# A two-layer decoder on one core: the opening's loads, one store, four transposes and the logarithm parts are moved

## The reference

```python
# layer 0, state space:   u = (x W_in2' + b) * sigmoid(x W_gate' + b_gate);  h_t = h_{t-1} A' + u_t B';  y = h C';  out = y W_out' + b_out
# layer 0, cross attention over 64 context tokens, 16 heads, with a mask
# layer 0, linear:        tanh(x W A1 A2 + bias)
# layer 1, local attention: scores from the cosine of g = x Wg' + bg, window of 128 tokens,
#     weighted with 1 / (mean + 0.5), softmax, times v = x Wv' + bv, then Wo
# layer 1, strided cross attention (4 keys a head)
# layer 1, feed forward: silu(q(x) q(Wg)') * (q(x) q(Wu)'), times q(Wd)', with q = rounding to 4-bit floats in blocks of 16
```

## Time and profile before

| | |
|---|---|
| median of 3 runs | 2803.29 us (2802.55 to 2804.59) |
| profiled execution | 2801.17 us |
| its span | 2799.6 us |
| PE busy | 2630.1 us (94%) |
| DVE, ACT, POOL busy | 1907.7, 808.7, 865.4 us |
| mean granted clock of PE | 0.978 |
| first stage | about 2 to 408 us |
| second stage | about 409 to 927 us |
| local attention | about 928 to 1600 us |

### The profile page before, as it was taken

One profiled execution on the slowest core, in us unless ns is written; L12 is line 12 of the kernel. 1 busy time (PEld: TensorE's weight loads), 2 busy tenths in 40 slices (PEclk: granted clock), 3 DMA queues, 4 the chain that ended last, 5 costly groups with the idle time before them and its releaser, 6 DMA issues. The chain is left out here.

```text
span 2799.6 us, 36866 instructions
## 1 busy us (share of the span) xinstructions
PE 2630.1 (94%) x13006; PEld 1586.6 (57%) x13006; DVE 1907.7 (68%) x3304; ACT 808.7 (29%) x1193; POOL 865.4 (31%) x902
## 2 busy tenths in 40 slices
PE   7999988999998889999998679999999999999996
PEld 3444534555555444444444346777777777777774
DVE  3688403666667336666678658888888888888884
ACT  1111312333332246666668511111111111111110
POOL 1232103554554346666667501111111111111000
PEclk9999989999999999999999989999999999999998
DMA  5344130000000133333335501111111111111111
GB/s 161 118 164 173 49 112 14 1 1 1 1 1 1 54 104 93 87 95 92 99 101 147 159 27 41 43 44 43 43 43 43 43 44 43 43 44 44 40 38 34
DMA packets 219395, 176.91 MB, mean 63 GB/s; under 512 B 38319, under 2 KB 184111, under 8 KB 218190
## 3 DMA queue, kind: packets, MB, share of 16 engines
q1 hardware_dynamic: 182230, 147.85, 17.6%
q10 hardware_dynamic: 36984, 26.71, 3.5%
HBM read 90.51 MB, written 52.43 MB: 51 GB/s over the span
## 5 line engine op out<-in xcount | busy, mean ns | idle before, releaser
L2016 PE MATMUL bank<-tiles,tl_XQT 128*128 128x512 f32 (+1 forms) x768 | 331.8, 575 | 7.6 <-DMA tl_XQT<-tl_QB 4.9
L2031 PE MATMUL bank<-tiles,tl_HT 128*128 128x512 f32 x704 | 316.3, 605 | 19.7 <-DMA tl_HT<-tl_tmp 19.7
L2021 PE MATMUL bank<-tiles,tl_XQT 128*128 128x512 f32 (+1 forms) x768 | 318.0, 557 | 0.0
L2031 PEld LDWEIGHTS bank<-tiles,tl_HT 128*128 128x128 f32 x704 | 225.2, 324 | 95.3 <-issue 28.0
L2016 PEld LDWEIGHTS bank<-tiles,tl_XQT 128*128 128x128 f32 x768 | 232.5, 310 | 74.0 <-issue 16.4
L2021 PEld LDWEIGHTS bank<-tiles,tl_XQT 128*128 128x128 f32 x768 | 236.7, 308 | 65.6 <-issue 0.2
L1376 POOL TENSOR_SCALAR_AFFINE_SELECT tiles<-tiles 128x512 f32<-128x512 f32 x256 | 179.5, 704 | 202.6 <-ACT tiles L1595 187.2
L1969 POOL TENSOR_TENSOR tl_rs<-tl_ve,mhalf 128x1 f32<-128x1 f32 x32 | 17.6, 549 | 593.0 <-DVE tl_ve L2124 593.0
L2065 ACT ACTIVATE tl_HQ<-bank 128x512 f32<-128x512 f32 (+1 forms) x96 | 53.9, 562 | 427.7 <-PE bank L2016 406.3
L1702 DVE SCALAR_TENSOR_TENSOR tiles<-tiles,bank 128x1024 f32<-128x1024 f32 (+1 forms) x128 | 141.7, 1148 | 25.2 <-PE bank L1475 25.2
L1381 POOL TENSOR_SCALAR_AFFINE_SELECT tiles<-tiles 128x512 f32<-128x512 f32 x224 | 152.6, 681 | 0.0
(11 more groups left out here) (279 smaller groups left out, 4961.1 us busy)
## 6 DMA issues: line engine op xcount, KB each, us to landing
tl_HT<-tl_tmp SPq DMA_DIRECT2D x256, 44.0 KB, 1.9
tl_HT<-tl_tmp ACTq DMA_DIRECT2D x256, 44.0 KB, 2.0
fp_weights<-space_quant ACTq DMA_DIRECT2D x33, 256.0 KB, 2.2
X<-in_x SPq DMA_DIRECT2D x8, 1024.0 KB, 12.0
v<-tiles SPq DMA_DIRECT2D x32, 256.0 KB, 2.4
unit_g<-tiles SPq DMA_DIRECT2D x32, 256.0 KB, 2.4
unit_gT<-tiles SPq DMA_DIRECT2D x32, 256.0 KB, 2.8
la_GN<-unit_g SPq DMA_DIRECT2D x128, 64.0 KB, 2.0
```

The source lines that it names most:

```text
L2016: mm = e.matmul(bank[(2 * q) % 3][:, 0:w], chunk(XQT[n % 2], c), WgT[q][:, :, c, :], start=(c == 0), stop=(c == C - 1))
L2021: mm = e.matmul(bank[(2 * q + 1) % 3][:, 0:w], chunk(XQT[n % 2], c), WuT[q][:, :, c, :], start=(c == 0), stop=(c == C - 1))
L2031: mm = e.matmul(bank[DOWN][:, :], chunk(HT, q), WdT[:, q, :], start=(q == 0), stop=(q == IC - 1))
```

## The change

It has five parts. In the first stage, the small loads, the output weights and the five bias columns move from ACT's queue to SP's: Bm and the small loads before the first FP4 unit, the others behind it, before x. The gate weights and the input weights are loaded in halves of 256 columns with a semaphore each, the gate weights' second half behind the two biases. The second folded store signals a kept semaphore, and SP waits for it in the second stage, just before it loads the local attention's weights. The transposes of the first four tiles of x go to banks 0 to 3, and only those from the sixth tile on wait for a copy. In the local attention `y_parts` goes from part 0 of its round to part 1 of the next, behind `norms`.

```diff
             def _(e):                                   # first stage, SP
                 e.dma_start(xT[0][:, :, :].rearrange("p c t -> p (c t)"), a["x_T"][0]).then_inc(s_xt[0].sem, 16)
-                e.dma_start(WiT[:, :, :], chunked(a["L0_attn_W_in_T"])[:, :, D:2 * D]).then_inc(s_wi.sem, 16)
+                for h in range(2):
+                    e.dma_start(WiT[:, :, h * D // 2:(h + 1) * D // 2],
+                                chunked(a["L0_attn_W_in_T"])[:, :, D + h * D // 2:D + (h + 1) * D // 2]).then_inc(s_wi[h].sem, 16)
                 e.dma_start(xT[1][:, :, :].rearrange("p c t -> p (c t)"), a["x_T"][1]).then_inc(s_xt[1].sem, 16)
...
+                e.wait_ge(s_zero.sem, s_zero.at(4))
+                e.dma_start(BmP[:, :, 0:ST], chunked(a["L0_attn_Bm_T"])).then_inc(s_bm.sem, 16)
+                for b in range(B):
+                    q = slice(QB * b, QB * b + ST)
+                    e.dma_start(Pw[0][q, q], a["L0_attn_A"]).then_inc(s_small.sem, 16)
+                    e.dma_start(PwT[0][q, q], a["L0_attn_A_T"]).then_inc(s_small.sem, 16)
+                    e.dma_start(CmP[:, :, q], chunked(a["L0_attn_Cm"])).then_inc(s_small.sem, 16)
                 load_weights(0)
+                e.dma_start(WoT[:, :, :], chunked(a["L0_attn_W_out_T"])).then_inc(s_wo.sem, 16)
+                for t, n in ((bk, "L0_xattn_bk"), (bq5, "L1_xattn_bq"), (bk5, "L1_xattn_bk"), (bv5, "L1_xattn_bv"), (lbv, "L1_attn_bv")):
+                    e.dma_start(t[:, :], columns_of(a[n]), allow_slow_non_contiguous=True).then_inc(s_cols.sem, 16)
                 for g in GROUPS:
...
-                e.dma_start(k.SW[:, VO_AT:FOLDED], w.VB).then_inc(s_out.sem, 16)
-                e.wait_ge(s_out.sem, s_out.at(32))
+                e.dma_start(k.SW[:, VO_AT:FOLDED], w.VB).then_inc(k.d_folded, 16)
+                e.wait_ge(s_out.sem, s_out.at(16))
...
-                    if g == 0 and m == 0:               # gate; inputs() likewise
-                        e.wait_ge(s_wg.sem, s_wg.at(16))
+                    if g == 0 and m % 2 == 0:
+                        e.wait_ge(s_wg[m // 2].sem, s_wg[m // 2].at(16))
...
             def _(e):                                   # first stage, ACT
-                e.dma_start(WgT[:, :, :], chunked(a["L0_attn_W_gate_T"])).then_inc(s_wg.sem, 16)
+                def gate_weights(h):
+                    x = slice(h * D // 2, (h + 1) * D // 2)
+                    e.dma_start(WgT[:, :, x], chunked(a["L0_attn_W_gate_T"])[:, :, x]).then_inc(s_wg[h].sem, 16)
+
+                gate_weights(0)
                 e.dma_start(bg[:, :], ...)              # and bi, as before
+                gate_weights(1)
                 e.wait_ge(s_bias.sem, s_bias.at(16 * 2))
...
+        x_bank = lambda n: n if n < B else XTB           # second stage
...
+                e.wait_ge(k.d_folded, 16)
                 e.dma_start(WgT[:, :, :], chunked(a["L1_attn_Wg_T"])).then_inc(s_next.sem, 16)
...
                 def transpose_x(n):
                     e.wait_ge(s_xe.sem, s_xe.at(n - 11))
-                    e.wait_ge(s_tc.sem, s_tc.at(n))
-                    transposed(x_tile(n), s_t)
+                    if n > B:
+                        e.wait_ge(s_tc.sem, s_tc.at(n))
+                    transposed(x_bank(n), x_tile(n), s_t)
...
+                    if part == 1 and batch_of(m) is not None:   # local attention, DVE, behind norms(m)
+                        y_parts(batch_of(m))
...
                     if part == 0:
                         if tile(m - 1):
                             unit(m - 1)
-                        b = batch_of(m)
-                        if b is not None:
-                            y_parts(b)
                         if tile(m):
                             biased(m)
```

More of the change, by code:

```diff
@@ L74, in __init__ @@
         self.done = []
+        self.d_folded = self.kept("folded_stored")
         self.d_w, self.d_wd = [self.kept(f"ffn_w{q}") for q in range(len(PIECES))], self.kept("ffn_w_down")
@@ L249, in ssm_and_weight_products @@
         bk, bq5, bk5, bv5, lbv = (sb(n, [P, C]) for n in ("bk", "bq5", "bk5", "bv5", "lbv"))
-        s_zero, s_const, s_small, s_wg, s_wi, s_bm, s_wo = (sem(n) for n in (
-            "zero", "one_row_made", "small", "w_gate", "w_in", "w_Bm", "w_out"))
+        s_zero, s_const, s_small, s_bm, s_wo = (sem(n) for n in ("zero", "one_row_made", "small", "w_Bm", "w_out"))
+        s_wg, s_wi = ([sem(f"w_{n}{h}") for h in range(2)] for n in ("gate", "in"))
         s_xt, s_x = [sem(f"xT_load{p}") for p in range(2)], [sem(f"x_load{g}") for g in GROUPS]
@@ L411, in inputs @@
                     e.wait_ge(s_u.sem, s_u.at(C * g + m - 1))
-                    if g == 0 and m == 0:
-                        e.wait_ge(s_wi.sem, s_wi.at(16))
+                    if g == 0 and m % 2 == 0:
+                        e.wait_ge(s_wi[m // 2].sem, s_wi[m // 2].at(16))
                     for c in range(C):
@@ L935, in _, with transposed @@
             def _(e):
-                def transposed(src, done):
+                def transposed(to, src, done):
                     for c in range(C):
-                        mm = e.transpose(bank[XTB][:, c * P:(c + 1) * P], src[:, c * P:(c + 1) * P], k.ident[:, :])
+                        mm = e.transpose(bank[to][:, c * P:(c + 1) * P], src[:, c * P:(c + 1) * P], k.ident[:, :])
                     mm.then_inc(done.sem, 1)
@@ L949, in transpose_x2 @@
                     e.wait_ge(s_xe.sem, s_xe.at(n))
-                    transposed(x_tile(n), s_xl)
+                    transposed(XTB, x_tile(n), s_xl)
                 def query(i):
@@ L1034, in _ @@
                         e.wait_ge(s_q.sem, s_q.at(C * (n // B - 1)))
-                        e.activation(XT[(n // B) % 2][:, :, (n % B) * P:(n % B + 1) * P], four(bank[XTB][:, :]), ACT.Copy).then_inc(s_tc.sem, 1)
+                        e.activation(XT[(n // B) % 2][:, :, (n % B) * P:(n % B + 1) * P], four(bank[x_bank(n)][:, :]), ACT.Copy).then_inc(s_tc.sem, 1)
                     if there(s - 2):
```

10 lines of the change are left out of this document (removed).

## The result

| | before | after |
|---|---|---|
| median of 4 runs each | 2802.92 us (2802.51 to 2804.59) | 2767.53 us (2766.48 to 2768.41) |
| profiled execution | 2801.17 us | 2768.34 us |
| its span | 2799.6 us | 2766.4 us |
| mean granted clock | 0.978 | 0.983 |

The ratio is 0.9872, with a 95% interval of 0.9855 to 0.989. The change is 35.4 us faster by the medians, where 28 was forecast. The direction was right and the size too small.

What follows compares the result with a forecast made beforehand. PE, nearly always busy, was taken to bound the kernel, other engines counting only where it waits. Gains 10.5 + 3.1 + 3.7 + 1.0 + 9.7 = 28.0 us led to 2775 us (own range 2770 to 2781; 8 in 10: 2769 to 2783).

Steps and rivals of the forecast that it cites:

- Opening: Start of the first stage: ACT's shorter queue and halved weights bring the third gate group earlier; gain 10.5 us (7 to 12).
- Store: First stage boundary: the end of the stage no longer waits for the last folded store; gain 3.1 us (2.7 to 3.4).
- Banks: Start of the second stage: transposes 1 to 4 need no copy before them; gain 3.7 us (3.2 to 4.2).
- Clock term: First query group of the second stage: the clock may rise near its start; gain 1.0 us (−0.3 to 2.1).
- Batches 1 and 2: Local attention: dots start 4.1 us earlier and 1.1 to 1.2 more is saved behind them; gain 5.3 us per batch.
- Batch 0: Local attention: PE's transposing would wait for the logarithm steps, ready only behind the norms; −0.9 us (−2 to 0).
- Batch 3: Local attention: steps and DVE's inverse only change order, PE waits as now for the scaled tile; 0 us (−1 to 1).
- The logarithm parts as a whole: Local attention, all four batches: moving the steps a round later gains 9.7 us (6 to 12).
- A: Opening: SP's queue becomes the limit as ACT's was, the opening gains 4 us, time 2782; chance 0.13.
- B: Local attention: the logarithm parts give nothing, this part gains 1 us, time 2784; chance 0.08.
- C: Whole kernel: steadier PE load lowers the granted clock; no gain from 1.1% less, 2814 at 1.5%; chance 0.03.
- D: Opening: bytes decide it, so it isn't earlier and gains 0, time 2786; chance 0.04.

Runs made afterwards that it cites:

- filled_transposes: Changed kernel with the first five tiles transposed through one bank again, plus four unread transposes behind each of these tiles; 2772.31 us.
- old_opening: Changed kernel with only the opening put back as before (small loads on ACT's queue, whole gate and input weights); 2779.76 us.
- fp4_first: Changed kernel with the first unit of the FP4 weights issued ahead of Bm and the small loads; 2768.38 us.
- filled_dots: Changed kernel with the logarithm steps early again, PE doing four overwritten 128x512 products where it would stand in batches 1 and 2; 2778.71 us.
- late_12: Changed kernel with the logarithm steps late in batches 1 and 2 only, in the old place in batches 0 and 3; 2771.47 us.
- y_early: Changed kernel with DVE's seven logarithm steps back in their old place in front of the bias addition; 2780.26 us.
- quarters_fp4: Changed kernel with gate and input weights in quarters instead of halves and the first FP4 unit ahead of the small loads; 2766.21 us.

## Why the prediction was right and where it was wrong

- **Opening, right.** Forecast: first gate group at 10.8, third at 28.3; measured 10.66 and 28.56, 11.0 gained (forecast 10.5). The first gate group took 6.32 where 5.4 was counted. SP's queue was quicker than counted (last small load at 16.00, forecast 18.9; FP4 weights at 21.6, forecast 23 to 24), so most of the 0.8 taken off for a late u or a late clock was not needed.
- **Store, right.** 3.1 forecast, 3.4 in after's trace, 2.8 when it alone is undone.
- **Banks, right in the sum, incomplete in the cause.** 3.7 forecast, 4.1 measured. At the full clock it is 3.7 (10.0 less 6.3 in the table of the boundary). What the step missed is that the transposes themselves run at either level of the clock: a set takes 1.09 at 0.50 and 0.63 at 1.00.
- **Clock term, wrong in size.** "I take 1.0 (−0.3 to 2.1)": 2.4 measured. The step weighed a rule of the Trainium skill ("TensorE: Matmul & The Clock Gate", "Part 4: PE-mode transpose") that transposes don't count as PE work against its opposite, and took the middle. The measurement contradicts the rule for these f32 transposes (the times that the Trainium skill gives there are of bf16 ones): in seven traces, after's among them, the clock went from 0.50 to 1.00 during nothing but transposes, and in filled_transposes 1.00 held through forty of them. The term came out even above the upper bound of 2.1, since that bound left a part of the group slow, and in after none was (3.70 us, against 6.08). That is one draw of several: with the clock back only inside the group, as in old_opening and fp4_first, the term is 1.5 to 1.7 (4.53 and 4.34 us), and within the bounds.
- **Batches 1 and 2, right in the sum, wrong in part of the cause.** 5.3 each forecast, 5.6 measured. The 4.1 of waiting is right for the dots' start (4.1 later in filled_dots), of which 3.8 to 3.9 is left behind the batch. The 1.1 to 1.2 behind it was put down to ACT's late square and table load beside the low clock; filled_dots shows that it is 1.7 to 1.8 and goes with the clock, with ACT as late as before.
- **Batch 0, wrong.** -0.9 forecast, 0 measured. The wait of 0.7 was foreseen; that the gate group behind it stands anyway was in no row that the step read. A wait was charged without looking at the next one on the same engine.
- **Batch 3, the step that failed most.** Forecast 0: "the steps and DVE's inverse only change order around the scores, and PE waits as now for the scaled tile". Measured 2.3, and this term alone is more than the 1.5 us by which the time lies below the range. Two things were missed: the early steps also stand in front of `la_AO` (1.10 us of PE; with the dots' shorter wait 0.7 us less waiting), and behind the idle time the clock was low, 1.6 us more. The second stood in the rows already quoted: the dots behind the wait took 2.00 us, those of an ordinary round 1.15. The 0.7 comes in every kernel with the edit. The 1.6 does not: late_12 has the early steps and loses only 0.8 in all, so this part hangs on where the clock falls. The logarithm parts as a whole, 13.5 to 13.6, lie outside the 6 to 12 that the prediction gave them.
- **The rivals.** A (SP's queue) did not come at this size but is next in line. B is refuted: the part that it put at 1 us is worth 13.5. C is refuted: the mean clock rose from 0.978 to 0.983. D, an opening that gains nothing, is refuted by the 11.0 that it gained.

The terms that failed have one thing in common: each wait taken from PE was priced at its own length plus a part, while in this kernel it mostly takes with it the low clock that follows. Over the span that is 2.4 us at the boundary, 3.5 in batches 1 and 2, and 1.6 in batch 3, 7.5 of some 35; of these the prediction had 1.0 and up to 2.3. The range was too narrow on that side: its low end was the sum with single terms off, and all the signs of error pointed the same way. Of the miss of 7.5, the trace has 6.5 behind batch 3, of which 1.3 are lost again in what follows; the last 2 to 3 are scatter between the profiled executions and the medians, which no step could have foreseen.

## What to carry to other kernels

Where PE is nearly always busy, price a wait that goes at its length plus what the rows behind it take more than the same rows elsewhere: here 1.7 us for 4.1 us of waiting, and 1.6 in batch 3, where 0.7 of waiting went. Give the second part a range down to zero, since the clock does not fall at the same place each time (0.8 in all in late_12). Before charging a new wait, read the next idle time of the same engine, which may swallow it. After removing the first bottleneck of an opening, see at once what is next: here halving paid 1.7 us and quartering nothing.

## What the runs showed of the hardware that was not expected

- Transposes in f32 against the identity (`PE ... ident,X 128x128`) bring the clock to its full level and hold it there: 0.50 to 1.00 at 398 in after, 1.00 from 394 to 401 in filled_transposes. Four of them take 1.09 us at 0.50 and 0.63 at 1.00 in these rows.
- After the idle time at the boundary (2 us; 2.4 and 4.8 in two) the clock fell in nine traces (0.50 from 395 in after) and did not in three (y_early, filled_transposes, quarters_fp4), with the same instructions around it in all but filled_transposes. From no fall to a rise within the query group it makes 2.4 us (6.3 to 8.7 in the table), which is of the size of the spread between runs of one kernel. The passage into the last block makes 2.6 to 3.5 us in the same way (five traces against the other nine).
- With large loads issued before it, the issue of a small load held its engine for 2.7 to 4.5 us (2.69 and 3.04 for SP in after, 4.47 in quarters_fp4), as it did on ACT (5.20), against 0.42 for others. What it costs depends on who waits for that engine. The row of quarters_fp4:

```profile
10.63 4.47 SPq L309 DMA_DIRECT2D ssm_Pw<-in_L_attn_A  x1
```
